# Attention's first batches among the last query tiles, projection weights in dead columns of y, and contiguous attention operands

## What is computed

```python
def _L0_attn_ref(hidden_states, Wq, Wk, Wv, Wo):
    q = (hidden_states @ Wq.T).reshape(B, Sq, H, HD).transpose(0, 2, 1, 3)
    k = (hidden_states @ Wk.T).reshape(B, Sq, HKV, HD).transpose(0, 2, 1, 3)
    v = (hidden_states @ Wv.T).reshape(B, Sq, HKV, HD).transpose(0, 2, 1, 3)
    ...
    qr = apply_rope(q, cos, sin)
    kr = apply_rope(k, cos, sin)
    ...
    scores = jnp.einsum('bhqd,bhkd->bhqk', qr, kr) / np.sqrt(HD) + mask
    attn = jax.nn.softmax(scores, axis=-1)
    out = jnp.einsum('bhqk,bhkd->bhqd', attn, v)
    out = out.transpose(0, 2, 1, 3).reshape(B, Sq, Dm)
    return out @ Wo.T

y = _L0_cond_ref(x, itok_B_8_3872, ...)
x = x + _L0_attn_ref(y, L0_attn_Wq, L0_attn_Wk, L0_attn_Wv, L0_attn_Wo)
x = x + _L0_ffn_ref(_L0_cond2_ref(x, ...), ...)
```

## Time and profile before

| | |
|---|---|
| median of three runs | 1007.97 us (1003.12 to 1008.37) |
| the profiled execution | 1006.78 us |
| its span, first to last instruction | 1004.8 us |
| PE busy | 934.7 us, 93% |
| DVE, ACT, POOL busy | 448.2, 209.3, 402.2 us |
| matmuls L754, L972, L1201 busy | 374.2, 323.6, 297.7 us |

### The profile page before, as it was taken

One profiled execution on the slowest core, in us unless ns is written; L12 is line 12 of the kernel. 1 busy time (PEld: TensorE's weight loads), 2 busy tenths in 40 slices (PEclk: granted clock), 3 DMA queues, 4 the chain that ended last, 5 costly groups with the idle time before them and its releaser, 6 DMA issues.

```text
span 1004.8 us, 23638 instructions
## 1 busy us (share of the span) xinstructions
PE 934.7 (93%) x10416; PEld 838.8 (83%) x10416; DVE 448.2 (45%) x895; ACT 209.3 (21%) x341; POOL 402.2 (40%) x295
## 2 busy tenths in 40 slices
PE   0899999899999999981899999999999999999997
PEld 0889899898888888861688888888898999999997
DVE  6555651002222222256876666666714344343344
ACT  4345542101000000012222222224312110110110
POOL 1244564004665656456477777776722000000000
PEclk9999999999999999995799999999999999999999
DMA  3688876011135221335225245443144112112101
GB/s 80 148 213 198 182 196 176 23 52 63 67 78 119 63 74 48 89 115 185 75 88 154 85 140 173 127 120 128 59 150 129 64 64 84 65 62 84 68 38 64
DMA packets 82053, 105.27 MB, mean 105 GB/s; under 512 B 41632, under 2 KB 56608, under 8 KB 81952
## 3 DMA queue, kind: packets, MB, share of 16 engines
q1 hardware_dynamic: 81440, 103.24, 35.5%
q0 software_dynamic: 512, 0.53, 0.2%
HBM read 74.08 MB, written 29.65 MB: 103 GB/s over the span
## 4 chain that ended last, share of the span: by engine, by line
PE 87%; DVE 5%; DMA 4%; issue 1%; SPq 1%; POOL 1%; ACT 1%; DVEq 0%
PE ps L754 21%; PE ps L972 20%; PE ps L1201 18%; PE ps L505 8%; PE ps L737 5%; PE ps L945 5%; PE ps L516 3%; PE ps L1169 3%; PE ps L925 2%; DMA wstage<-in_dram 1%; DVE wo_lo L855 1%; DMA toep<-kpad 1%; PE ps L1221 1%; DMA kpad<-ksb 1%; PE ps L1222 1%
## 5 line engine op out<-in xcount | busy, mean ns | idle before, releaser
L1201 PE MATMUL ps<-wb,xf 128*128 128x420 f32 (+1 forms) x1152 | 195.2, 329 | 2.4 <-DVE wb L1254 1.9
L1201 PEld LDWEIGHTS ps<-wb,xf 128*128 128x128 f32 x1152 | 189.4, 188 | 5.3 <-issue 3.0
L754 PE MATMUL ps<-y_hi,w_hi 128*128 128x512 f32 x320 | 124.9, 390 | 0.0
L754 PE MATMUL ps<-y_lo,w_hi 128*128 128x512 f32 x320 | 124.7, 390 | 0.0
L754 PE MATMUL ps<-y_hi,w_lo 128*128 128x512 f32 x320 | 124.6, 390 | 0.0
L972 PE MATMUL ps<-wo_hi,ot_hi 128*128 128x512 f32 x256 | 110.2, 430 | 2.8 <-issue 2.8
L505 PE MATMUL ps<-xc,toep 64*128 64x192 f32 (+4 forms) x1088 | 99.6, 335 | 11.8 <-DMA toep<-kpad 8.2
L972 PE MATMUL ps<-wo_hi,ot_lo 128*128 128x512 f32 x256 | 110.2, 430 | 0.0
L505 PEld LDWEIGHTS ps<-xc,toep 64*128 64x128 f32 x1088 | 91.8, 191 | 15.8 <-issue 12.4
L972 PE MATMUL ps<-wo_lo,ot_hi 128*128 128x512 f32 x256 | 103.2, 403 | 0.0
L1021 POOL TENSOR_TENSOR sc<-sc,stat 128x1024 f32<-128x1024 f32 x32 | 61.7, 1927 | 82.8 <-DVE stat L1017 82.8
(11 more groups left out here) (145 smaller groups left out, 1399.7 us busy)
## 6 DMA issues: line engine op xcount, KB each, us to landing
toep<-kpad SPq DMA_DIRECT2D x64, 272.0 KB, 4.7
xc<-in_dram SPq DMA_DIRECT2D x32, 256.0 KB, 5.1
q_rows<-rf SPq DMA_DIRECT2D x32, 256.0 KB, 2.5
q<-q_rows SPq DMA_DIRECT2D x16, 512.0 KB, 4.8
xr<-in_dram SPq DMA_DIRECT2D x16, 512.0 KB, 5.3
x_scratch<-xr SPq DMA_DIRECT2D x16, 512.0 KB, 2.9
x<-x_scratch SPq DMA_DIRECT2D x16, 512.0 KB, 3.6
out_dram<-x SPq DMA_DIRECT2D x15, 512.0 KB, 2.6
```

What stands on the lines that cost most here:

```text
L754: mm = pe.matmul(ps[:, 4 * (m % 2) + g, :], w[a][:, j, :], yt[b][:, j, g * 512:(g + 1) * 512], start=(j == 0 and a + b == 0), stop=(j == N ...
L1201: mm = pe.matmul(joint_bank(i, piece)[:, 0:hi - lo], xf[i % 2][:, a, t, :], wb[t][:, c, lo:hi], start=(t == 0 and a + c == 0), stop=(piece ...
```

## The change

- **Order of the tiles.** The last three query weight tiles (m = 7, 8, 9) are run by token group: for each g the three m. `TAIL` is 28, the first of these twelve tiles; they rotate through banks 4 to 7 (`kq_bank`). All q rows of token group 0 are complete after tile 30.
- **First units between them.** With `lead` = n - 33, PE runs scores 0, 1, 2 in front of tiles 33, 34, 35, values 0 in front of 37, scores 3 in front of 38, values 1 in front of 39, then scores 4; DVE, POOL and ACT have the softmax steps of these units among the ropes. The attention loops begin at step 2 (`FIRST`).
- **Projection weights in dead columns.** When a token group's last tile has been read, its columns of y are free. The output projection's weights (raw, high, low), `ot`, `xr`, `craw`, `pr`, `mix` and the first x1 buffer lie in such columns. A raw tile is loaded to the place where its low part will be, and the low part is made in place; there is no staging ring and no wait for one. Loads 0 to 3 are issued behind the load of q for pair 0, 4 to 7 once tile 33 is through. The dense layer's weights are also loaded to the place of their low part.
- **Contiguous operands.** `ot` holds each replica's 128 columns side by side, and `probs` is read with the positions innermost. o_hi and o_lo are two operations each of 256 elements. `mix` is in two halves.

The diff, cut to its core:

```diff
+        QTOK = TOK // 4
+        y_cols = [p[:].rearrange("p j b s -> p j (b s)") for p in y]
+
+        def wo(part, t):
+            return y_cols[part][:, 2 * (t % 4):2 * (t % 4) + 2, t // 4 * QTOK:(t // 4 + 1) * QTOK]
+        def wo_raw(t):
+            return raw_cols[:, 2 * (t % 4):2 * (t % 4) + 2, t // 4 * QTOK:(t // 4 + 1) * QTOK]
+
+        def ot(part, i):
+            return y_cols[part][:, 2 * (i % 2):2 * (i % 2) + 2, 2 * QTOK:3 * QTOK]
...
-        A, Z = NU - 2, NU - 1
-        ORDER = [(m, g) for m in range(A) for g in range(4)] + \
-                [(A, 0), (Z, 0), (A, 1), (A, 2), (A, 3), (Z, 1), (Z, 2), (Z, 3)]
-        N_Z0, N_A3 = ORDER.index((Z, 0)), ORDER.index((A, 3))
+        Z = NU - 1
+        TAIL = 4 * (NU - 3)
+        ORDER = [(m, g) for m in range(NU - 3) for g in range(4)] + [(m, g) for g in range(4) for m in range(NU - 3, NU)]
+        N_Z = [ORDER.index((Z, g)) for g in range(4)]
+        LEAD = N_Z[1]
 
         def next_weights(n):
 
-            return Z if n == 4 * A - 2 else n // 4 + 1 if n % 4 == 0 and n // 4 + 1 < Z else None
+            return {TAIL - 2: NU - 2, TAIL: NU - 1}.get(n, n // 4 + 1 if n % 4 == 0 and n < TAIL else None)
+
+        def kq_bank(n):
+            m, g = ORDER[n]
+            return bank(4 * (m % 2) + g) if n < TAIL else bank(4 + (n - TAIL) % 4)
+
+        def tile_done(eng, n):
+            m, g = ORDER[n]
+            if g < 3:
+                eng.wait_ge(pe_m, sum(other < 3 for _, other in ORDER[:n + 1]))
...
-                if (m, g) == (Z, 2):
-                    sp.wait_ge(pe_unit, NU)
-                    for t in range(WS3):
+                if i == LEAD + 1:
+                    tile_done(sp, LEAD)
+                    for t in range(4, NQT):
                         load_w3(sp, t)
+                if i == LEAD + 3:
+                    load_kv(sp, 2)
+                    load_q(sp, 2)
+                if i == 4 * NU - 1:
+                    sp.wait_ge(pe_unit, NU + 1)
+                    sp.dma_start(cidx_i[:], cond.partition_broadcast(P)).then_inc(ld_cond, 16)
+                    load_residual(sp, 0)
+                    load_residual(sp, 1)
+                    load_kv(sp, 3)
+                    load_q(sp, 3)
...
                     for last in range(n - SR + 1, n + 1):
                         stored(sp, last)
                     load_q(sp, 0)
-                    sp.wait_ge(pe_unit, NU - 1)
+                    for t in range(4):
+                        load_w3(sp, t)
                     load_q(sp, 1)
...
+                lead = n - LEAD
+                if 0 <= lead < CR:
+                    scores(pe, lead)
+                if lead in (4, 6):
+                    values(pe, (lead - 4) // 2)
+                if lead == 5:
+                    scores(pe, CR)
...
+                elif n < TAIL:
+                    pe.wait_ge(v_rcos, n - 7)
                 else:
-                    if 4 * (m - 2) + g + 1 > 0:
-                        pe.wait_ge(v_rcos, 4 * (m - 2) + g + 1)
+                    pe.wait_ge(v_rcos, max(n - 3, TAIL - 7 + (n - TAIL)) if n >= TAIL + 4 else n - 7)
-                        mm = pe.matmul(ps[:, 4 * (m % 2) + g, :], w[a][:, j, :], yt[b][:, j, g * 512:(g + 1) * 512],
+                        mm = pe.matmul(kq_bank(n), w[a][:, j, :], yt[b][:, j, g * 512:(g + 1) * 512],
...
+            for t in range(4):
+                wo_hi(act, t)
             exponentials(act, 0)
             exponentials(act, 1)
+            exponentials(act, 2)
+            for t in range(4, NQT):
+                wo_hi(act, t)
...
+                if 0 <= lead < CR:
+                    scale_and_max(v, lead)
+                if lead in (1, 2):
+                    sums(v, lead - 1)
+                if lead == 3:
                     turn_probs(v, 0)
-                    scale_and_max(v, 2)
-                    sums(v, 1)
-                m_ready(v, n)
+                if lead in (4, 6):
+                    o_lo(v, (lead - 4) // 2)
+                    turn_probs(v, (lead - 4) // 2 + 1)
+                    sums(v, (lead - 4) // 2 + 2)
+                if lead in (5, 6):
+                    scale_and_max(v, lead - 2)
+                for t in WO_LO_V.get(lead, ()):
+                    wo_lo(v, t)
+                tile_done(v, n)
...
+                lead = n - LEAD
+                if 0 <= lead < CR:
+                    subtract_max(gp, lead)
+                if 1 <= lead <= CR:
+                    normalise(gp, lead - 1)
+                if lead == 5:
+                    subtract_max(gp, CR)
+                if lead == 6:
+                    normalise(gp, CR)
+                for t in WO_LO_G.get(lead, ()):
+                    wo_lo(gp, t)
...
+        WO_GP = (3, 5, 7)
+        WO_LO_V = {2: (0,), 3: (1, 2), 5: (4,), 6: (6,)}
+        WO_LO_G = {3: (3,), 4: (5,), 6: (7,)}
...
+            act.wait_ge(ld_w3[t], 16)
+            act.activation(wo(0, t), wo_raw(t), ACT.Copy).then_inc(a_w3, 1)
 
         def wo_lo(eng, t):
             eng.wait_ge(a_w3, t + 1)
-            ins = eng.tensor_tensor(wo[1][:, t, :], wstage3[t % WS3][:], wo[0][:, t, :].bitcast(F32), ALU.subtract)
+            ins = eng.tensor_tensor(wo(1, t), wo_raw(t), wo(0, t).bitcast(F32), ALU.subtract)
+            sp.dma_start(wo_raw(t), w_o[:, t, :].rearrange("p (n c) -> p n c", n=2)).then_inc(ld_w3[t], 16)
...
-                if i + 3 < NPAIR:
+                if 1 <= i < NPAIR - 3:
                     load_kv(sp, i + 3)
                     load_q(sp, i + 3)
-                if i == 8:
-                    for t in range(WS4):
-                        load_w4(sp, t)
-                if i == 12:
-                    load_w4(sp, WS4)
+                if i in (6, 8, 10, 12):
+                    load_w4(sp, (i - 6) // 2)
...
-            for t in range(WS4 + 1, WB_EARLY):
+            sp.wait_ge(pe_o, NUNIT)
+            for t in range(WB_FREE, WB_EARLY):
                 load_w4(sp, t)
...
-            probs = pt[:].rearrange("p (g r j q) -> p g j q r", g=4, r=REP, j=2)
+            probs = pt[:].rearrange("p (g r j q) -> p g r j q", g=4, r=REP, j=2)
...
-                                       probs[rows, g, j, :, :], start=(j == 0), stop=(j == late))
+                                       probs[rows, g, :, j, :], start=(j == 0), stop=(j == late))
...
+        def o_banks(G):
+
+            return ps[:, 2 * G:2 * G + 2, 256:384].rearrange("p h (r q) -> p h r q", q=HB)
+
+        def o_heads(part, u, G):
...
+            return ot(part, u // 2)[:, G, :].rearrange("p (r h q) -> p h r q", r=REP, h=4)[:, 2 * b:2 * b + 2, :, :]
+
+        def o_hi(act, u):
+            act.wait_ge(pe_o, u + 1)
+            if u >= 4:
+                act.wait_ge(pe_y, 2 * (u // 2 - 1))
+            act.activation(o_heads(0, u, 0), o_banks(0), ACT.Copy)
+            act.activation(o_heads(0, u, 1), o_banks(1), ACT.Copy).then_inc(a_othi, 1)
+
+        def o_lo(v, u):
+            v.wait_ge(a_othi, u + 1)
+            v.tensor_tensor(o_heads(1, u, 0), o_banks(0), o_heads(0, u, 0).bitcast(F32), ALU.subtract)
+            v.tensor_tensor(o_heads(1, u, 1), o_banks(1), o_heads(0, u, 1).bitcast(F32), ALU.subtract).then_inc(v_otlo, 1)
...
-                if i > 0:
+                if i == 0:
+                    pe.wait_ge(v_rcos, 4 * NU - 1 + n)
+                else:
                     pe.wait_ge(a_pr, 2 * (i - 1) + n + 1)
...
-                heads = ot[a][:, i % 2, t // REP, :, :, t % REP].rearrange("p h q -> p (h q)")
-                mm = pe.matmul(ps[:, 6 + n, :], heads, wo[c][:, t, n * 512:(n + 1) * 512],
+                heads = ot(a, i)[:, t // REP, t % REP * P:(t % REP + 1) * P]
+                mm = pe.matmul(ps[:, 6 + n, :], heads, wo(c, t)[:, n, :],
...
-            scores(pe, 2)
-            pe.wait_ge(v_rcos, 4 * NU)
+            scores(pe, CR + 1)
             for w in STEPS:
                 i, n = w // 2 - 1, w % 2
-                if i >= 0:
-                    project(pe, i, n, 0)
+                project(pe, i, n, 0)
...
-            act.wait_ge(pe_unit, NU + 1)
+            o_hi(act, 0)
+            o_hi(act, 1)
+            exponentials(act, CR)
-                if w >= 3:
+                if w > FIRST:
                     take_projection(act, (w - 1) // 2 - 1, (w - 1) % 2)
```

More of the change, by code:

```diff
@@ L184, in build, with spare @@
         Q_AT = ROPE_AT + (2 * RR + SR) * 512
-        s3 = ExitStack()
[L187 to L196, removed]
+        QTOK = TOK // 4
+        y_cols = [p[:].rearrange("p j b s -> p j (b s)") for p in y]
+        def wo(part, t):
+            return y_cols[part][:, 2 * (t % 4):2 * (t % 4) + 2, t // 4 * QTOK:(t // 4 + 1) * QTOK]
+        over = ExitStack()
+        take(over, "y_hi_again", [P, Y_END // 2])
+        raw_cols = take(over, "raw_cols", [P, NJ, TOK])
+        over.close()
+        def wo_raw(t):
+            return raw_cols[:, 2 * (t % 4):2 * (t % 4) + 2, t // 4 * QTOK:(t // 4 + 1) * QTOK]
+        def ot(part, i):
```

(25 more changed lines are left out.)

136 lines of the change are left out of this document (44 added, 92 removed).

## The result

The changed kernel takes 952.5 us in the median of four runs (951.98 to 954.01), the kernel before 1007.3 beside it on the same chip: a ratio of 0.9466, 95% interval 0.9436 to 0.9496. The forecast was 972 with a range of 962 to 982, so the change won 54.8 us where 35 were expected. The question is where the other 20 came from.

What follows compares the result with a forecast made beforehand. PE was taken as the bound, by its idle and slow-clock hole at the hand-over and the price of each matmul elsewhere: 1006.8 - 22.6 (hole) - 12.4 (stationary operand) = 971.8, said as 972, range 962 to 982.

Steps and rivals of the forecast that it cites:

- Change 2: Contiguous operands in attention: 12.4 us from project's weight loads and matmul pace, nothing from the values' moving operand.
- The bound of 3 us: Limits on the gain from the values' contiguous moving operand: 0 and -0.1 per unit, 3 us in all.
- Contiguous stationary operand: Project matmuls reading `ot` contiguously: shorter weight loads and faster pace, a gain of 12.4 us.
- The hole: Hand-over from query projection to attention, where PE idles and the clock drops: new order gains 22.6 us.
- the walk: Stepping the four engine queues through the new order at the hand-over: waits of 6.7 us, scores 6 at 475.3.
- The clock: Matmuls slowed by clock drops after PE's waits of 2.5 and 2.7 at the hand-over: 3 us.
- How long DVE is held: DVE's wo_lo waiting on POOL at the hand-over: let in within the rope pair, gain 26.3 before clock and q load.
- DVE is starved: Rival: DVE held through POOL's rope pairs at the hand-over; hole 17.2, time 977; chance 0.22.
- light: Rival: light hand-over with DVE hardly held; hole 27.3, time 967; chance 0.18.
- The rival on them: Half operations of o_hi and o_lo cost as much as whole ones: 972 + 12 = 984; chance 0.05.
- the slower case: Values to o_hi to o_lo to scores lasts 3.6 us or more, losing the gain: 1010 or more; chance 0.03.
- Attention's end and the dense layer: Weight loads from attention's end into the FFN keep their distance to PE's last project: change of 0.

Runs made afterwards that it cites:

- e3: The changed kernel with both operands (`ot` and `probs`) in the old layout, leaving the new tile order and the weights in dead columns: 981.9 us.
- e1: The changed kernel with project's stationary operand `ot` alone put back to a step of four elements: 960.0 us.
- e4: The kernel before with contiguous `probs` alone, `ot` in its old layout, and the result copies in two halves: 984.2 us.
- e2: The changed kernel with the values' moving operand alone read 64 elements apart again: 970.3 us.
- after: The changed kernel itself, with all parts of the change: 952.5 us.
- e8: The changed kernel with the sums of batches 2 and 3 on DVE ahead of the rope and o_lo: 950.3 us.
- e11: The changed kernel with the sums earlier on DVE and each gather issued behind POOL's subtract: 945.1 us.
- e7: The changed kernel with each gather issued on POOL behind the subtract instead of ahead of it: 948.9 us.

## Why the prediction was wrong, point by point

**The step that failed** is the end of "Change 2": "Values' moving operand also becomes contiguous. I cost it at nothing". Its yardstick was that the strided values take no longer per column than the scores' contiguous 64-column matmuls. As arithmetic that holds: on the busiest row group 8 values matmuls have 1024 columns in 1.58 us, 1.5 ns each, and 8 scores 512 in 0.84, 1.6 each. But it compares two things with different limits. Contiguous values do the same 1024 columns in 0.87 us, 0.85 ns each, so the scores were never at the price of a column and can't tell what one costs; what does bound them isn't shown. The bound of 3 us rested on the same yardstick and fell with it: 0.70 a unit in 32 units is 22 us, and e3 to e1, and e4 in the kernel before, measured 21.9 and 22.1. The rows that would have served stood in the trace. L754's 128x512 matmuls with contiguous moving operand cost 0.227 for 512 columns, 0.44 ns each. The values have two records for each matmul (x1536 above), so their busiest row group has 16 records or 2048 columns in 1.58 us, 0.77 ns each; at 0.44 they would take 0.91 us. That is an estimate from rows of before alone, it gives 0.7 a unit or 22 us in all, and the runs showed 0.87. With it the forecast would have been 950.

**Contiguous stationary operand.** Forecast 12.4 us, measured 11.6 (e3 to e2); 0.44 a unit forecast, 0.41 seen. The weight loads show 313 ns in e1 and 189 in e2 with the same 128 columns. The Trainium skill, TensorE: Matmul & The Clock Gate, section "LDWEIGHTS", whose rule would have made this part worth nothing, isn't borne out here: the measurement decides.

**The hole.** Forecast 22.6 us, alone 24.4 (e3), in after 26.4 on the span. Scores 0 began at 407.69 without a wait, so the 0.7 for the load of q was not needed. The tiles ended at 452.17 for the forecast's 453.4, and from there to scores 6 lie 22.9 us: 13.8 of work (2 x 1.05, 2 x 1.09 and 42 x 0.227), 5.7 of waits, and so 3.4 for the clock. The forecast had waits of 1.5, 2.5 and 2.7 at values 2, scores 5 and values 3; they were 1.8, 1.1 and 2.8. In e2, whose values cost what the walk had, they were 1.0, 2.6 and 1.4, 5.0 in all for the 6.7: the places are right and the sum is 1.7 too high. The clock was put at 3 in two drops. In after there were two, but behind values 2 and values 3 (granted clock 0.56 from 457.7 to 461.6 and 0.53 from 471.5 to 475.1), none behind scores 5; and as e8 and e11 show the same waits with and without such a drop, that the size came out near is partly luck. The 2.9 that four cheaper units of values bring (1.81 to 1.09) belong to the failed step.

**How long DVE is held.** This was the forecast's widest unknown, and it decided between it and its first two rivals. The rows (start us, us):

```profile
429.88 4.01 DVE L903 TENSOR_TENSOR y_lo<-raw_cols,y_hi 128x1024 fp32r<-128x1024 f32 x2
...
442.87 2.12 DVE L903 TENSOR_TENSOR y_lo<-raw_cols,y_hi 128x1024 fp32r<-128x1024 f32 x1
...
457.85 3.14 DVE L903 TENSOR_TENSOR y_lo<-raw_cols,y_hi 128x1024 fp32r<-128x1024 f32 x1
```

```profile
440.26 2.40 POOL L903 TENSOR_TENSOR y_lo<-raw_cols,y_hi 128x1024 fp32r<-128x1024 f32 x1
442.62 1.29 POOL L874 TENSOR_TENSOR rot<-rot,cst 128x512 f32<-128x512 f32 x1
443.99 2.14 POOL L878 TENSOR_TENSOR rf<-rot,rc 128x512 f32<-128x512 f32 x1
446.09 2.39 POOL L903 TENSOR_TENSOR y_lo<-raw_cols,y_hi 128x1024 fp32r<-128x1024 f32 x1
```

wo_lo 4 on DVE waited through L874 and ended at 444.99; in return POOL's L878, 1.29 us elsewhere, took 2.14. So DVE was let in between the two operations of the rope, as the walk had it (it said 445.7), and wasn't held to the end of POOL's busy stretch. The rival "DVE is starved" fell, and so did "light": 3.14 and 2.12 are well over 1.2. No run took POOL's own wait between the two operations away, so that this gap is what lets DVE in stays argued.

**Half operations.** o_hi took 0.39 and 0.38, o_lo 0.41 and 0.41: no wait of scores on them in the steady units. The rival on them fell, and with it the slower case. e1 shows how much room there was: its halves, written four elements apart, take 0.64, 0.69, 0.65 and 0.65 us, 2.3 from the first start to the last end, and its scores don't wait in the steady units either.

**Attention's end and the dense layer.** Forecast 0: from the dense matmul that waited for the last split weights to the end 231.9 us before (1004.8 - 772.9) and 232.4 after (951.2 - 718.8). Right within half a microsecond.

**The sum.** 35.0 forecast; plus 22 for the values, plus about 2 for the hole, less 0.8 for `ot`, less 4.5 for the gathers: 53.7, where the span lost 53.6. That it closes to a tenth is luck, since the medians it is made of are good to a microsecond or two.

## What to carry to other kernels

To learn what a layout costs, compare with a row that is bound by the same thing: set the time per column beside the cheapest column in the trace, and not beside a row of small matmuls that may be bound by something else; and count the columns by the trace's records, not by the kernel's matmuls. Here the float32 moving operand of values wanted its neighbours adjacent (1.8 times the time at a step of 64 elements, nearly all regained by pairs), and so, for less, did the float32r stationary operand of project (a load of 311 ns at a step of four, 190 contiguous). And when a stage gets faster, look at what its companions do at that moment: here gathers that cost nothing beside slow matmuls cost 4.5 us beside fast ones, and moving them by one POOL operation brought the unit step back to 7.60.

## What the runs showed of the hardware that was not expected

- A 32x128 values matmul whose moving operand lay 64 elements apart: 24 of them (48 records) 1.58 us; in runs of two 0.92; contiguous 0.87.
- A gather issued by POOL (0.98 us) whose end fell among those 48 records, contiguous, stopped PE's weight loads once for up to 0.20 us; one that started with them (e1) or 1.8 us behind them (e7) didn't, nor did one beside strided values (e2).
- Where DVE and POOL compete, both pay: DVE's 1.2-us operation ended after 2.1 to 3.1 us, and the POOL operation that it slipped in ahead of took 2.14 instead of 1.29. The Trainium skill, SBUF — State Buffer, section "SBUF: two separate sides", has the shared pair taken for a whole instruction at a time; these rows agree, while the earlier trace rows show a wait through three.
- Equal idle times of PE didn't always cost clock: after waits of 0.3 and 2.8 us the granted clock stayed at 1.00 in e8 and had a mean of 0.83 in e11.
